# Attention on one core: one pair's bias added by VectorE, norm arguments moved to GpSimd, a set of score products moved ahead of the turned outputs

## The chip, the cores and the metric

The kernel runs on 1 core of one Trainium2 chip. The metric is the device time of one execution in microseconds, as the median of the timed runs. TensorE multiplies matrices into PSUM, VectorE and ScalarE work on PSUM and SBUF, GpSimd on SBUF; SyncE issues DMAs. Each engine runs its own instructions in order, and they meet at semaphores.

## The reference

The input is 32 sequences of 256 tokens with 128 features. Four blocks follow one another, each with a residual: attention with an MLP, a mixture of 8 experts (2 per token), a gated recurrence, and the experts again. The change is in the first block:

```python
xn = _layernorm(x, ln1_g, ln1_b)                 # of an x that is normed already
q, k, v = split(xn @ in_proj_w.T + in_proj_b)    # 16 heads of 8 features
mask = _causal_mask(s, rel_pos)                  # per head: a bias by distance, -inf above the diagonal
scores = einsum('bhqd,bhkd->bhqk', q, k) / sqrt(8) + mask
o = einsum('bhqk,bhkd->bhqd', softmax(scores), v)
x = x + o @ out_w.T + out_b
xm = _layernorm(x, ln2_g, ln2_b)
return x + relu(xm @ w1.T + b1) @ w2.T + b2
```

## The kernel before

The attention block is a software pipeline over the 32 sequences. Every engine has a `body(b)`, written out by hand, that is called for b from -4 to 39; one call is a pass here. The order of calls in it is the order of the engine's instructions, and nothing else sets it. A pass works on several sequences at once: the scores of sequence b, the maxima of b+1, the projections of b+2 and b+3, the output of b-1, the MLP of b-2 and b-3, and the dispatch to experts behind that.

The 16 heads are taken as 8 pairs, j = 0 to 7. A score tile of a pair is 128x768: for each of two heads the three 128x128 blocks on and under the diagonal. Each pair is computed twice:

- **For the maxima.** `bias_for_max` turns the bias into `max_banks` with six 128x128 matmuls, `for_max` adds the products, ScalarE copies the tile to `copied` (`copy_for_max`), and VectorE folds the copies to one maximum per query and head (`fold_keys`, `fold_half`, `fold_on`, `reduce_max`). The maxima go back into q by a DMA.
- **For the scores.** `for_scores` writes `score_banks`, VectorE adds the mask into `ebuf` (`add_mask`, L1153), ScalarE takes the exponential, and `weigh` multiplies by v.

`fill` (L866 and L853 are its first products) issues one pair of scores and one pair of the next sequence's maxima together. There is one `score_banks` and one `max_banks`, so each set waits for the set before to be taken out of both: `scores_free` is raised by VectorE's mask, `maxed_free` by ScalarE's copy. In `fill(b, 0, .., b+1, 3)` the pair for the maxima is number 3; the next set, `fill(b, 1, .., b+1, 4)`, needs that one copied.

`turn(b-1)` (L918, L923) transposes the weighted outputs that ScalarE's `take_O` has copied to `outT`; VectorE's `normalise` (reciprocal L1162, then two products) reads them. TensorE issues it between the third set (scores 2) and the fourth (scores 3).

Three norms run in a pass. For each, VectorE takes `bn_stats` and `bn_aggr`, then the argument var + eps with a small `tensor_scalar` (L1084 and L1085 for the first, L1195 for the second, L1228 for the rows of the experts), and GpSimd raises it to -1/2 (`roots`, `second_root`, `row_root`) and applies it. GpSimd also issues the indirect DMAs that scatter rows to the experts (L1694).

Of the kernel before, what the change touches and what calls it, by code (L numbers as in the profile page):

```python
# [19 lines left out]
P = 128  # L20
# [295 lines left out]
def attention(nc, ctx, s, ins, xres, ident, identb, w, z, region, share, slots_dram, pads_dram):  # L316
# [35 lines left out]
    neghalf = sb("neghalf", [P, 4])  # L352
# [287 lines left out]
    mv = sb("mv", [P, RING, 2, 2])  # L640
    arg = sb("arg", [P, 2, 2])
    rs = sb("rs", [P, RING, 2, 2])
# [23 lines left out]
    stats3, mv3, arg3, rs3 = sb("stats3", [P, 2, 6]), sb("mv3", [P, 2, 2]), sb("arg3", [P, 2]), sb("rs3", [P, 2])  # L666
# [11 lines left out]
    def bankW(lo=0, hi=512):  # L678
# [5 lines left out]
    spread, max_spread = sem("spread"), sem("max_spread")  # L684
    hi_ready, lo_ready, folded, max_ready = sem("hi_ready"), sem("lo_ready"), sem("folded"), sem("max_ready")
    exped, weighed, O_taken = sem("exp_done"), sem("pv_done"), sem("O_taken")
    arg1_ready, rs1_ready, xn_ready, xlb_ready, xl_ready = (sem("arg1_ready"), sem("rs1_ready"), sem("xn_ready"),
                                                            sem("xlb_ready"), sem("xl_ready"))
    arg2_ready, rs2_ready = sem("arg2_ready"), sem("rs2_ready")
    xm_ready, ysum_ready = sem("xm_ready"), sem("ysum_ready")  # L690
    xm_high, arg3_ready, rs3_ready, d_normed = sem("xm_high"), sem("arg3_ready"), sem("rs3_ready"), sem("d_normed")
# [46 lines left out]

    EARLY = 8 + 3

    def banks_of_max(c, j):

        g = 8 * c + j
        return score_banks if g < EARLY and g % 2 == 1 else max_banks

# [20 lines left out]
    with nc.Block() as block:  # L766

        @block.tensor
        def _(pe):
# [45 lines left out]

            def bias_for_max(c, j):
# [3 lines left out]
                max_banks = banks_of_max(c, j)  # L820
# [3 lines left out]
                for hh in range(2):  # L824
                    h = 2 * j + hh
                    nc.tensor.matmul(max_banks[:, hh, 0:P], biasb[:, h, P:2 * P], identb[:], start=True, stop=False,  # L826
                                     skip_group_check=True)
                    nc.tensor.matmul(max_banks[:, hh, P:2 * P], biasb[:, h, 0:P], identb[:], start=False, stop=False,  # L828
                                     skip_group_check=True)
                    nc.tensor.matmul(max_banks[:, hh, 2 * P:BK], biasb[:, h, 0:P], identb[:], start=False, stop=False,  # L830
                                     skip_group_check=True)
# [217 lines left out]
            for b in BODIES:  # L1049
                body(b)  # L1050
# [6 lines left out]
        def _(dve):  # L1057
# [3 lines left out]
            def norm_stats(c):  # L1061
# [6 lines left out]
                if 2 * c in X_PARTS:  # L1068
                    dve.wait_ge(x_in[X_PARTS.index(2 * c)], 16)
# [1425 lines left out]
```

## Time and profile before

| | |
|---|---|
| time, median of 3 runs | 1423.78 us (1423.7 to 1432.5) |
| span of the profiled execution | 1524.2 us |
| granted clock, mean over the span | 0.890 |
| busy, share of the span: TensorE, VectorE, ScalarE, GpSimd | 80%, 75%, 63%, 65% |
| attention loop, first and last reciprocal L1162 | 86.0 and 677.9 us |

The profiled execution has its own time: of it the page gives the span, from the first to the last instruction, and that is longer than the timed runs. The attention loop fills about the first 45% of it; the experts, the recurrence and the experts again follow. An operation's duration in the trace includes its start and its drain, so two neighbours on one engine overlap by some 0.08 us.

### The profile page before, as it was taken

To read this page: it belongs to the slowest core of one execution; us is meant where nothing else is said; L and a number is where in the kernel's file an instruction comes from. 1 tells how busy PE (TensorE), PEld (TensorE's weight loads), DVE (VectorE), ACT (ScalarE), POOL (GpSimd) and SP (SyncE) were. 2 spreads that over 40 slices of the span, in tenths; PEclk is the share of its full clock that TensorE was granted. 3 is DMA by queue.
4 is the path that set the end of the run, shared out by engine and by line. 5 is a ranking of instruction groups with operands and counts; after the bars stand their busy time and mean duration, and the time that the engine had idled before them with its cause. 6 is when DMAs were issued, how large, how long until landed. Compare 5 with 4: busy or idle time off the path is not lost. (4 is left out here: it accounts for less than half of the span.)

```text
span 1524.2 us, 38116 instructions
## 1 busy us (share of the span) xinstructions
PE 1216.6 (80%) x11689; PEld 1017.3 (67%) x11689; DVE 1144.1 (75%) x3833; ACT 967.7 (63%) x2078; POOL 991.9 (65%) x1131
## 2 busy tenths in 40 slices
PE   5889999999999999973788888577787449888850
PEld 3667777777777777753788888455566348788850
DVE  5489999999999999965566665488888546666638
ACT  3588888888888888851555544277777435455420
POOL 4346688888888888777355665237777835666530
PEclk9699999999999999995799997588878669999955
DMA  7211111111111111123222222112222122222228
GB/s 199 86 46 46 48 60 60 60 60 60 59 60 60 60 60 60 39 93 83 73 86 86 81 85 68 49 49 83 73 83 69 45 68 84 86 84 84 77 83 277
DMA packets 99443, 117.19 MB, mean 77 GB/s; under 512 B 17784, under 2 KB 79792, under 8 KB 99248
## 3 DMA queue, kind: packets, MB, share of 16 engines
q1 hardware_dynamic: 70560, 73.57, 16.3%
q0 software_dynamic: 16896, 35.16, 6.8%
q10 hardware_dynamic: 11792, 6.05, 1.4%
q8 instruction: 98, 1.61, 0.5%
q14 instruction: 97, 0.79, 0.2%
HBM read 47.56 MB, written 41.51 MB: 58 GB/s over the span
## 5 line engine op out<-in xcount | busy, mean ns | idle before, releaser
L1153 DVE TENSOR_TENSOR ebuf<-score_banks,region 128x768 f32<-128x768 f32 x256 | 243.6, 951 | 18.8 <-PE score_banks L862 13.1
L1402 ACT ACTIVATE region<-ebuf 128x768 f32<-128x768 f32 x256 | 215.9, 860 | 23.0 <-DVE ebuf L1153 23.0
L1380 ACT CAST copied<-max_banks 128x768 bf16<-128x768 f32 x251 | 201.9, 804 | 15.1 <-PE max_banks L850 12.5
L1842 POOL DMA_INDIRECT choice_rows<-second_yo,second_xg x136 | 133.1, 979 | 112.7 <-PE second_by L1880 69.3
L1842 POOL DMA_INDIRECT choice_rows<-first_yo,first_xg x136 | 130.7, 961 | 114.0 <-PE first_by L1880 65.9
L1694 POOL DMA_INDIRECT expert_rows<-d_rows,a_d_index x112 | 129.4, 1155 | 27.9 <-issue 17.2
L1918 ACT ACTIVATE second_silu<-second_bgu,second_biases 128x256 f32<-128x256 f32 (+1 forms) x144 | 61.0, 466 | 114.3 <-PE second_bgu L1871 66.7
L1918 ACT ACTIVATE first_silu<-first_bgu,first_biases 128x256 f32<-128x256 f32 (+1 forms) x144 | 61.9, 462 | 111.8 <-issue 83.6
L1954 DVE SCALAR_TENSOR_TENSOR second_hT<-second_bgu,second_biases,second_silu 128x256 f32<-128x256 f32 (+1 forms) x144 | 62.1, 464 | 70.3 <-ACT second_silu L1918 37.6
L905 PE MATMUL bankO<-region,vaug 128*32 128x256 f32 (+1 forms) x2048 | 111.1, 334 | 1.9 <-ACT region L1402 1.9
L853 PE MATMUL max_banks<-region_r 32*128 32x256 f32 x502 | 98.3, 388 | 11.9 <-DVE ebuf L1153 7.4
L826 PE MATMUL max_banks<-identb,region 128*128 128x128 bf16 x502 | 100.4, 225 | 4.8 <-ACT copied L1380 4.7
L1954 DVE SCALAR_TENSOR_TENSOR first_hT<-first_bgu,first_biases,first_silu 128x256 f32<-128x256 f32 (+1 forms) x144 | 62.9, 465 | 54.9 <-ACT first_silu L1918 36.1
L866 PE MATMUL score_banks<-region_r 32*128 32x256 f32 x512 | 99.1, 384 | 3.0 <-DVE ebuf L1153 2.9
L1880 PE MATMUL second_by<-region,second_hT 128*128 x544 | 79.3, 289 | 27.4 <-DVE second_hT L1954 23.5
L828 PE MATMUL max_banks<-identb,region 128*128 128x128 bf16 x502 | 99.5, 223 | 0.0
L830 PE MATMUL max_banks<-identb,region 128*128 128x128 bf16 x502 | 99.4, 223 | 0.0
L1880 PE MATMUL first_by<-region,first_hT 128*128 x544 | 82.6, 298 | 17.5 <-DVE first_hT L1954 15.0
L1869 PE MATMUL first_bgu<-first_xhi,first_whi 128*128 128x256 f32 (+1 forms) x288 | 93.5, 325 | 0.6 <-issue 0.6
L1583 POOL TENSOR_TENSOR rs<-arg,neghalf 128x4 f32<-128x4 f32 x32 | 37.1, 1160 | 86.0 <-DVE arg L1085 86.0
L1880 PEld LDWEIGHTS second_by<-region,second_hT 128*128 128x128 f32 x544 | 69.7, 199 | 34.3 <-issue 34.2
L1869 PE MATMUL second_bgu<-second_xhi,second_whi 128*128 128x256 f32 (+1 forms) x288 | 90.5, 314 | 0.4 <-DVE second_xlo L1945 0.2
(369 smaller groups left out, 4531.6 us busy)
## 6 DMA issues: line engine op xcount, KB each, us to landing
region_r<-region_r SPq DMA_DIRECT2D x192, 128.0 KB
first_xg<-expert_rows SPq DMA_DIRECT2D x64, 132.0 KB
second_xg<-expert_rows SPq DMA_DIRECT2D x64, 132.0 KB
z_rows<-choice_rows SPq DMA_DIRECT2D x32, 256.0 KB
c_rows<-choice_rows SPq DMA_DIRECT2D x16, 512.0 KB
out<-xres ACTq DMA_DIRECT2D x16, 256.0 KB
choice_rows<-first_yo,first_xg POOLq DMA_INDIRECT x136
choice_rows<-second_yo,second_xg POOLq DMA_INDIRECT x136
```

Of the source, the lines that this page charges most:

```text
L826: nc.tensor.matmul(max_banks[:, hh, 0:P], biasb[:, h, P:2 * P], identb[:], start=True, stop=False, skip_group_check=True)
L828: nc.tensor.matmul(max_banks[:, hh, P:2 * P], biasb[:, h, 0:P], identb[:], start=False, stop=False, skip_group_check=True)
L905: last = nc.tensor.matmul(bankO[VW * i:VW * (i + 1), g // 2, out:lo + 2 * P], vaug[:, n, kt, h, :], p32[:, (h // 2) % 4, h % 2, cols], sta ...
L1153: nc.vector.tensor_tensor(ebuf[:, half_of_ebuf(c, j), :, :], score_banks[:, :, 0:BK], bias32[:, plain(j), :], ALU.add).then_inc(scores_fre ...
L1380: nc.scalar.copy(copied[:, 2 * j:2 * j + 2, :], banks_of_max(c, j)[:, :, 0:BK]).then_inc(maxed_free, 1)
L1402: nc.scalar.activation(p32[:, j % 4, :, :], ebuf[:, half_of_ebuf(c, j), :, :], ACT.Exp).then_inc(exped, 1)
L1694: pool.indirect_dma_start(slots_dram, bass.IndirectOffsetOnAxis(ap=d.index[:, m % 2, k, t:t + 1], axis=0), d.rows[:, (2 * m + t // 2) % DE ...
L1842: pool.indirect_dma_start(choice_dram, bass.IndirectOffsetOnAxis(ap=xg[:, i % G, t, E:E + 1].bitcast(I32), axis=0), yo[:, i % 4, t, :], No ...
L1869: nc.tensor.matmul(dst, wh[:, at], xhi[:, i % 2, 0:n], start=True, stop=False)
L1880: last = nc.tensor.matmul(by[i % 2][:, t * E:(t + 1) * E], hT[:, i % 4, f, t * P:(t + 1) * P], w["down"][:, bass.ds(e, 1), f, :].rearrange ...
L1918: nc.scalar.activation(act_[:, f, 0:T(i) * P], bgu[i % 2 * NF + f][:, 0:T(i) * P], ACT.Silu, bias=biases[:, i % 4, f:f + 1]).then_inc(silu ...
L1954: nc.vector.scalar_tensor_tensor(hT[:, i % 4, f, 0:T(i) * P], bgu[i % 2 * NF + f][:, 2 * P:(2 + T(i)) * P], biases[:, i % 4, NF + f:NF + f ...
```

## The change

It has three parts. Pair 3 gets its bias for the maxima from VectorE: a table `bias_rows` is made once, TensorE issues no bias matmuls for that pair, ScalarE doesn't copy it, and VectorE's `add_for_max` writes `copied` from the bank and the table. The arguments of the norms move to GpSimd, where `roots` also takes the place of `row_root`. And `fill(b, 3, ..)` is issued ahead of `turn(b-1)`.

```diff
--- before.py
+++ after.py
@@ -349,7 +349,9 @@
-    neghalf = sb("neghalf", [P, 4])
+    MAX_ON_DVE = (3,)
+    bias_rows = sb("bias_by_queries", [P, 2 * len(MAX_ON_DVE), BK], BF16)
+    neghalf = sb("neghalf", [P, 6])
...
@@ -813,22 +823,26 @@
+            def turn_bias(banks, j):
+                for hh in range(2):
+                    h = 2 * j + hh
...
             def bias_for_max(c, j):
 
                 if not exists(c):
                     return
-                max_banks = banks_of_max(c, j)
                 copied = 8 * c + j - 1 if 8 * c + j < EARLY else 8 * c + j
                 if some(copied):
                     pe.wait_ge(maxed_free, copied)
-                for hh in range(2):
...
+                if j not in MAX_ON_DVE:
+                    turn_bias(banks_of_max(c, j), j)
...
@@ -1025,8 +1039,8 @@
                 project_kv(b + 2)
                 mlp_T(b - 2)
                 fill(b, b % RING, 2, b + 1, (b + 1) % RING, 5)
+                fill(b, b % RING, 3, b + 1, (b + 1) % RING, 6)
                 turn(b - 1)
-                fill(b, b % RING, 3, b + 1, (b + 1) % RING, 6)
                 weigh(b, b % RING, 0)
...
@@ -1046,7 +1060,13 @@
+            for q, j in enumerate(MAX_ON_DVE):
+                if q:
+                    pe.wait_ge(rows_taken, q)
+                turn_bias(bankO, j).then_inc(rows_full, 1)
             for b in BODIES:
+                if b == 0:
+                    pe.wait_ge(rows_taken, len(MAX_ON_DVE))
                 body(b)
...
@@ -1076,13 +1098,7 @@
-                    last = ch.mark(nc.vector.bn_aggr(mv[:, n, t, :], stats[:, t, :]))
-                ch.wait(last)
-
-                if some(c):
-                    dve.wait_ge(rs1_ready, c)
-                nc.vector.tensor_scalar(arg[:, 0, :], mv[:, n, :, 1], 1.0, EPS, ALU.mult, ALU.add)
-                nc.vector.tensor_scalar(arg[:, 1, :], mv[:, n, :, 1], 1.0 + EPS, EPS * EPS, ALU.mult, ALU.add).then_inc(arg1_ready, 1)
+                    nc.vector.bn_aggr(mv[:, n, t, :], stats[:, t, :]).then_inc(mv_ready, 1)
...
@@ -1140,6 +1156,19 @@
+            def add_for_max(c, j):
+
+                if not exists(c):
+                    return
+                dve.wait_ge(maxed_full, 8 * c + j + 1)
+                if some(8 * c + j):
+                    dve.wait_ge(maxed_free, 8 * c + j)
+                if some(c):
+                    dve.wait_ge(folded, len(FOLDS) * (c - 1) + fold_of(j) + 1)
+                at = slice(2 * MAX_ON_DVE.index(j), 2 * MAX_ON_DVE.index(j) + 2)
+                nc.vector.tensor_tensor(copied[:, 2 * j:2 * j + 2, :], banks_of_max(c, j)[:, :, 0:BK], bias_rows[:, at, :],
+                                        ALU.add).then_inc(maxed_free, 1)
...
@@ -1301,6 +1327,7 @@
                 fold_half(b + 1, 0)
                 add_mask(b, 0)
                 finish(b - 3)
+                add_for_max(b + 1, 3)
                 members(b - 5)
                 row_stats(b - 3)
                 add_mask(b, 1)
...
@@ -1374,8 +1405,10 @@
                 act.wait_ge(maxed_full, 8 * c + j + 1)
-                g = sum(j >= past for first, past in FOLDS)
-                if some(c) and j == FOLDS[g][0]:
+                if j - 1 in MAX_ON_DVE:
+                    act.wait_ge(maxed_free, 8 * c + j)
...
@@ -1468,7 +1501,6 @@
                 exponentials(b - 1, 7)
-                copy_for_max(b + 1, 3)
                 exponentials(b, 0)
                 copy_for_max(b + 1, 4)
...
@@ -1572,26 +1604,35 @@
+            def roots(c, r):
+
+                n, lo, hi = c % RING, 0 if exists(c) else 2, 4 if exists(r) else 2
+                if exists(c):
+                    pool.wait_ge(mv_ready, 2 * c + 2)
...
+                    ch.mark(nc.gpsimd.tensor_scalar(arg[:, 4:6], mv[:, n, 0:2, 1], 1.0 + EPS, EPS * EPS, ALU.mult, ALU.add))
+                if exists(r):
+                    pool.wait_ge(mv3_ready, 2 * r + 2)
...
+                ch.step(nc.gpsimd.tensor_scalar(arg[:, lo:hi], mv[:, n, lo:hi, 1], 1.0, EPS, ALU.mult, ALU.add))
...
+                nc.gpsimd.tensor_tensor(rs[:, n, lo:hi], arg[:, lo:hi], neghalf[:, lo:hi], ALU.pow).then_inc(rs_ready, 1)
...
@@ -1617,7 +1658,8 @@
-                pool.wait_ge(arg2_ready, c + 1)
+                pool.wait_ge(mv2_ready, 2 * c + 2)
+                ch.step(nc.gpsimd.tensor_scalar(arg2[:], mv2[:, :, 1], 1.0, EPS, ALU.mult, ALU.add))
                 nc.gpsimd.tensor_tensor(rs2[:], arg2[:], neghalf[:, 0:2], ALU.pow).then_inc(rs2_ready, 1)
...
@@ -1726,9 +1761,9 @@
                 biased_input(b - 1)
-                row_root(b - 3)
                 norm_apply(b + 3, (b + 3) % RING)
-                roots(b + 4, (b + 4) % RING)
+                if exists(b + 4) or exists(b - 3):
+                    roots(b + 4, b - 3)
```

TensorE at the start of a pass, from the first set to the bias of the second; before:

```order
L826 MATMUL max_banks<-identb,region 128x128 [waits maxed_free]
L828 MATMUL max_banks<-identb,region 128x128
L830 MATMUL max_banks<-identb,region 128x128
L826 MATMUL max_banks<-identb,region 128x128
L828 MATMUL max_banks<-identb,region 128x128
L830 MATMUL max_banks<-identb,region 128x128
L853 MATMUL max_banks<-region_r 128x256 [waits scores_free,max_spread]
L853 MATMUL max_banks<-region_r 128x256
```

and now, from the same set to the second set's bias:

```order
L867 MATMUL max_banks<-region_r 128x256 [waits scores_free,max_spread,maxed_free]
L867 MATMUL max_banks<-region_r 128x256
L880 MATMUL score_banks<-region_r 128x256 x2
L864 MATMUL max_banks<-region_r 128x128 x2
L876 MATMUL score_banks<-region_r 128x128 x2
L1002 MATMUL bankTW<-w,hT 128x128 x4
L919 MATMUL bankO<-region,vaug 32x256 [waits exp_done]
L919 MATMUL bankO<-region,vaug 32x256 x3
L919 MATMUL bankO<-region,vaug 32x128 x4
L829 MATMUL max_banks<-identb,region 128x128 [waits maxed_free]
```

The first set has lost its six bias matmuls and carries their wait; the bias of the next set still waits for `maxed_free`.

TensorE around the turned outputs (`outT`), before:

```order
L853 MATMUL max_banks<-region_r 128x256 x2
L866 MATMUL score_banks<-region_r 128x256 x2
L850 MATMUL max_banks<-region_r 128x128 x2
L862 MATMUL score_banks<-region_r 128x128 x2
L918 MATMUL bankTW<-ident,outT 128x128 x4
L923 MATMUL bankTW<-ident,outT 128x128 x4
L826 MATMUL max_banks<-identb,region 128x128
L828 MATMUL max_banks<-identb,region 128x128
L830 MATMUL max_banks<-identb,region 128x128
```

and now:

```order
L829 MATMUL max_banks<-identb,region 128x128
L831 MATMUL max_banks<-identb,region 128x128
L833 MATMUL max_banks<-identb,region 128x128
L867 MATMUL max_banks<-region_r 128x256 x2
L880 MATMUL score_banks<-region_r 128x256 x2
L864 MATMUL max_banks<-region_r 128x128 x2
L876 MATMUL score_banks<-region_r 128x128 x2
L932 MATMUL bankTW<-ident,outT 128x128 x4
L937 MATMUL bankTW<-ident,outT 128x128 x4
```

The bias and products of the fourth set stand ahead of the turned outputs.

VectorE from the mask of set 0 to the low part of xm, before:

```order
L1153 TENSOR_TENSOR ebuf<-score_banks,region 128x768
L1202 TENSOR_TENSOR xres<-bankTW,ysum 128x256
L1219 BN_STATS stats<-xres 128x6 x2
L1153 TENSOR_TENSOR ebuf<-score_banks,region 128x768
L1226 BN_AGGR mv<-stats 128x2 x2
L1228 TENSOR_SCALAR arg<-mv 128x2
L1209 TENSOR_TENSOR xmlo<-bankTW,xmhi 128x256
```

and now:

```order
L1182 TENSOR_TENSOR ebuf<-score_banks,region 128x768
L1229 TENSOR_TENSOR xres<-bankTW,ysum 128x256
L1169 TENSOR_TENSOR copied<-max_banks,bias_by_queries 128x768
L1247 BN_STATS stats<-xres 128x6 x2
L1182 TENSOR_TENSOR ebuf<-score_banks,region 128x768
L1254 BN_AGGR mv<-stats 128x2 x2
L1236 TENSOR_TENSOR xmlo<-bankTW,xmhi 128x256
```

The add into `copied` stands behind the finished rows (`xres`) and ahead of the statistics; the argument of the rows is gone.

## Rows read from the trace of the kernel before

**Rows 1.** Stretch table: us; busy of TensorE, its weight loads, VectorE, ScalarE, GpSimd; clock; DMA.

```profile
418.00:456.00 38.00, 35.70 (x474) 28.24 (x473) 35.88 (x100) 33.13 (x62) 33.14 (x41) 1.00 0.18 60
```

**Rows 2.** Waits, 200 to 560 us: who waited for whom, total, times, longest.

```profile
POOL rs L1583 <- DVE arg L1085: 19.1, 19, 1.7
...
PE bankTW L918 <- ACT outT L1411: 11.8, 18, 0.7
```

**Rows 3.** Timeline of VectorE: start, us, line, operation, tiles, [idle before <-releaser].

```profile
426.43 0.48 DVE L1092 SCALAR_TENSOR_TENSOR region_r<-bankTW,bqk,region_r 128x256 fp32r<-128x256 f32 x1 [0.43 <-ACT region_r L1356]
...
428.17 0.41 DVE L1202 TENSOR_TENSOR xres<-bankTW,ysum 128x256 f32<-128x256 f32 x1
...
429.31 0.96 DVE L1153 TENSOR_TENSOR ebuf<-score_banks,region 128x768 f32<-128x768 f32 x1 [0.21 <-PE score_banks L862]
...
430.46 0.47 DVE L1228 TENSOR_SCALAR arg<-mv 128x2 f32<-128x2 f32 x1
431.03 0.42 DVE L1209 TENSOR_TENSOR xmlo<-bankTW,xmhi 128x256 fp32r<-128x256 f32 x1
...
433.10 0.36 DVE L1162 RECIPROCAL rden<-bankTW 128x32 f32<-128x32 f32 x1
...
435.50 0.17 DVE L1084 TENSOR_SCALAR arg<-mv 128x2 f32<-128x2 f32 x1
...
435.65 0.55 DVE L1119 TENSOR_TENSOR fold<-copied 128x768 bf16<-128x768 bf16 x1
...
439.01 0.96 DVE L1153 TENSOR_TENSOR ebuf<-score_banks,region 128x768 f32<-128x768 f32 x1
...
445.64 0.48 DVE L1092 SCALAR_TENSOR_TENSOR region_r<-bankTW,bqk,region_r 128x256 fp32r<-128x256 f32 x1 [0.24 <-ACT region_r L1356]
```

**Rows 4.** Timeline of TensorE, the same pass, same columns.

```profile
428.35 0.23 PE L826 MATMUL max_banks<-identb,region 128*128 128x128 bf16 x1
...
428.79 0.38 PE L853 MATMUL max_banks<-region_r 32*128 32x256 f32 x2
...
431.90 0.66 PE L918 MATMUL bankTW<-ident,outT 128*128 128x128 f32 x4 [0.65 <-ACT outT L1411]
432.39 0.60 PE L923 MATMUL bankTW<-ident,outT 128*128 128x128 f32 x4
...
433.26 0.38 PE L853 MATMUL max_banks<-region_r 32*128 32x256 f32 x2
...
433.63 0.86 PE L905 MATMUL bankO<-region,vaug 128*32 128x256 f32 x16
...
440.52 0.38 PE L853 MATMUL max_banks<-region_r 32*128 32x256 f32 x2
```

**Rows 5.** Timeline of ScalarE, the same pass.

```profile
430.62 0.38 ACT L1421 CAST xmhi<-bankTW 128x256 fp32r<-128x256 f32 x1
...
431.71 0.83 ACT L1380 CAST copied<-max_banks 128x768 bf16<-128x768 f32 x1
```

**Rows 6.** Groups of instructions, VectorE and ScalarE, 200 to 560 us: count, busy, mean.

```profile
L1153 DVE TENSOR_TENSOR ebuf<-score_banks,region 128x768 f32<-128x768 f32 x149 | 141.7, 951 | 6.8 <-PE score_banks L862 3.7 <-ACT region L1402 2.0 <-issue 0.5
...
L1228 DVE TENSOR_SCALAR arg<-mv 128x2 f32<-128x2 f32 x18 | 8.8, 490 | 0.6
...
L1195 DVE TENSOR_SCALAR arg<-mv 128x2 f32<-128x2 f32 x18 | 3.0, 169 | 0.6
...
L1380 ACT CAST copied<-max_banks 128x768 bf16<-128x768 f32 x148 | 119.2, 805 | 1.6
```

**Rows 7.** Timeline of GpSimd, the same pass.

```profile
429.82 1.09 POOL L1694 DMA_INDIRECT expert_rows<-d_rows,a_d_index  x1 [0.18 <-issue]
```

**Rows 8.** Table of stretches, the first passes (clock behind the busy times).

```profile
88.00:92.00 4.00, 2.95 (x44) 1.78 (x41) 3.90 (x11) 2.94 (x4) 2.49 (x3) 0.86 0.02 4
92.00:96.00 4.00, 4.00 (x51) 2.93 (x44) 3.29 (x7) 3.14 (x8) 0.26 (x1) 0.71 0.00 0
```

More of the change, by code:

```diff
@@ L744, in banks_of_max, with fold_of @@
         return score_banks if g < EARLY and g % 2 == 1 else max_banks
+    def fold_of(j):
+        return sum(j >= past for first, past in FOLDS)
     def group(c):
@@ L845, in for_max @@
             def for_max(c, n, j, second):
-                max_banks = banks_of_max(c, j)
+                max_banks, alone = banks_of_max(c, j), j in MAX_ON_DVE
                 for hh in range(2):
@@ L1182, in second_norm @@
                 dve.wait_ge(W_free, useW("att", c) + 1)
+                if some(c):
+                    dve.wait_ge(mv2_ready, 2 * c)
                 for t in range(2):
@@ L1190, in second_moments @@
                 for t in range(2):
-                    last = ch.mark(nc.vector.bn_aggr(mv2[:, t, :], stats2[:, t, :]))
-                ch.wait(last)
-                if some(c):
-                    dve.wait_ge(rs2_ready, c)
-                nc.vector.tensor_scalar(arg2[:], mv2[:, :, 1], 1.0, EPS, ALU.mult, ALU.add).then_inc(arg2_ready, 1)
+                    nc.vector.bn_aggr(mv2[:, t, :], stats2[:, t, :]).then_inc(mv2_ready, 1)
             def finish(c):
@@ L1225, in row_moments @@
                 for t in range(2):
-                    last = ch.mark(nc.vector.bn_aggr(mv3[:, t, :], stats3[:, t, :]))
-                ch.wait(last)
-                nc.vector.tensor_scalar(arg3[:], mv3[:, :, 1], 1.0, EPS, ALU.mult, ALU.add).then_inc(arg3_ready, 1)
+                    nc.vector.bn_aggr(mv[:, row_slot(c), 2 + t, :], stats3[:, t, :]).then_inc(mv3_ready, 1)
             def sort(c):
@@ L1321, in body @@
                 add_mask(b, 4)
+            for q in range(len(MAX_ON_DVE)):
+                dve.wait_ge(rows_full, q + 1)
+                nc.vector.tensor_copy(bias_rows[:, 2 * q:2 * q + 2, :], bankO[:, :, 0:BK]).then_inc(rows_taken, 1)
+            dve.wait_ge(rows_taken, len(MAX_ON_DVE))
             for b in BODIES:
@@ L1376, in copy_for_max @@
                 act.wait_ge(maxed_full, 8 * c + j + 1)
-                g = sum(j >= past for first, past in FOLDS)
-                if some(c) and j == FOLDS[g][0]:
+                if j - 1 in MAX_ON_DVE:
+                    act.wait_ge(maxed_free, 8 * c + j)
+                g = fold_of(j)
+                if some(c) and j == min(i for i in range(*FOLDS[g]) if i not in MAX_ON_DVE):
                     act.wait_ge(folded, len(FOLDS) * (c - 1) + g + 1)
@@ L1652, in residuals @@
                                         xb2[:].rearrange("p t e -> p (t e)"), ALU.add).then_inc(ysum_ready, 1)
-            def row_root(c):
-                if not exists(c):
-                    return
-                pool.wait_ge(arg3_ready, c + 1)
-                if some(c):
-                    pool.wait_ge(d_normed, c)
-                nc.gpsimd.tensor_tensor(rs3[:], arg3[:], neghalf[:, 0:2], ALU.pow).then_inc(rs3_ready, 1)
             def row_apply(c):
```

69 lines of the change are left out of this document (38 added, 31 removed).

## The prediction, made before the changed kernel had run

> **What bounds the kernel now.** I read the table of stretches first, then the waits, then the timelines of the engines over one pass of the attention loop. In the steady stretch no engine stands out: in 38 us TensorE is busy 35.70 us and VectorE 35.88, at a granted clock of 1.00, the 2.4 GHz level [rows 1]. Shares don't say what a microsecond on either is worth, so I looked for the chain that closes from one pass to the next. TensorE waits once a pass for outT, ahead of the turned outputs (18 waits, 11.8 us) [rows 2]; VectorE waits for ScalarE's upper q (0.43 at 426.43) and for the products of set 1 (0.21 at 429.31) [rows 3]. The two hand the chain to each other.
>
> One pass of VectorE [rows 3] and TensorE [rows 4] gives it. Call F the moment at which TensorE starts the products of the pass's second set (L853 at 428.79). Ahead of F, VectorE takes q at 426.43, then come a fold and the mask of set 0, and the finished rows at 428.17. TensorE doesn't wait there: its bias matmuls start at 428.35. Behind F, VectorE adds the mask of set 1 at 429.31 (F+0.52), takes the reciprocal for the turned outputs at 433.10 (F+4.31) and adds the mask of set 5 at 439.01. That ends at 439.97 and releases TensorE's seventh set, from which project_q and the next q follow. The pass takes 19.21 us from q to q (426.43 to 445.64). So what is put into this chain lengthens the pass; time taken off an engine beside it gives nothing.
>
> **The change, part by part.**
>
> *The add on VectorE.* Once a pass ScalarE loses a 128x768 copy (mean 805 ns) and VectorE gains an add of the same shape out of PSUM; the mask add, also out of PSUM, has a mean of 951 ns [rows 6]. Bounds: 0.80 us as the copy, 0.95 as the mask add; I take 0.95, the same engine and operation with one narrower operand and a narrower result. TensorE loses six bias matmuls, 0.44 us from the first to the products (428.35 to 428.79) [rows 4].
>
> What decides is who waits for the add. The bias of the next maxima needs max_banks empty, and it stands ahead of the second set's products in TensorE's queue; queued behind it are k, v, the turned xm and, through these, all that ScalarE does next. The add stands behind the finished rows: it can't start before 428.17 + 0.41 = 428.58, nor end before 429.53. With a hand-over of 0.03 (as from xmhi's end at 431.00 to xmlo at 431.03 [rows 3, 5]) the bias starts at 429.56 instead of 428.35, and F moves to 430.0: **+1.2 us a pass**. With 0.80 us it would be 1.05; nothing or a gain is excluded, since the bias can't start before the bank is read. TensorE's saved 0.44 lies in front of this wait and is worth nothing. VectorE has only row_stats to do meanwhile, then it waits for set 1 too.
>
> *The turned outputs behind the fourth set.* The fourth set's bias needs ScalarE's copy of the maxima of pair 5, which started at 431.71 and took 0.83, so it ended at F+3.75 [rows 5]. ScalarE stands in one row from the values to that copy, all of it behind F, so this moment goes with F. The fourth set can start at F+3.8, its products 0.44 later at F+4.2, and the turn 0.37 after those (433.26 to 433.63, where the next matmuls follow now), at F+4.6. The turn takes 432.39 + 0.60 - 431.90 = 1.09 us [rows 4], to F+5.7, and the reciprocal comes then instead of at F+4.31: **+1.4 us a pass**. Bounds: 0 (if VectorE comes to the reciprocal that late for another reason) and 1.5. VectorE can't do the mask of set 3 first: it stands behind the reciprocal and the outputs. The fourth set itself gains 0.25 us (F+4.47 to F+4.2), and nobody is waiting for that.
>
> *The roots' arguments.* VectorE loses four small operations a pass. The two for the first norm, from 435.50 with the wait ahead of them to the fold at 435.65 [rows 3], lie on the chain: **-0.25** with that wait, 0.15 without. The second norm's lies ahead of the wait for q, which swallows its 0.17. The row argument (L1228) averages 490 ns against 169 for the second norm's of the same shape (L1195) [rows 6]; here it ran from 430.46 to 430.93, and GpSimd's indirect DMA instruction, from 429.82, ended at 430.91 [rows 7]. But what follows it is xmlo at 431.03, and that needs xmhi, which ends at 431.00 [rows 5]. So by the rows it is worth nothing.
>
> The Trainium skill (SBUF — State Buffer, the section on the engine side) says that VectorE and GpSimd share a pair of SBUF ports as an exclusive lock, held for the whole instruction. By that rule the 0.3 us between the two means would be given back, some 10 us in all, and the sum would be about 1478; the rows agree that VectorE was held, but not that anyone waited for it.
>
> GpSimd gains three small operations and loses one pow a pass; it waited 19.1 us for the argument in 19 passes [rows 2], 1.0 a pass, which covers up to 0.3 each. If that cover were gone, the next to be late would be xm, needed behind F, which itself comes later. Cost 0. The one-time bias table is six matmuls and a copy, 0.44 + 0.95 and hand-overs: 0 to 2 us, I take 1. SyncE's queue is untouched.
>
> *Slack.* The mask of set 5 ended at 439.97 and the seventh set's products started at 440.52 [rows 3, 4], so up to 0.5 us of delay is swallowed if TensorE has that reserve in every pass, and 0 if it has none; I take **-0.25**.
>
> *Sum.* 1.2 + 1.4 - 0.25 - 0.25 = 2.1 us a pass. Thirty passes (1 to 30 of 32) have both the add and the turn: 63 us. Four at the ends have only one of them: 2 us. With the table 66 us, so the profiled execution would go from 1524.2 to 1590 us. The median of the timed runs, 1423.78, lies 100 us (7%) under this span. If the loop was as long there, I add 66; if it was shorter in proportion, 62. I take the middle: **1488 us**.
>
> **Rivals.**
>
> *Only the add counts.* If VectorE comes to the reciprocal no earlier than F+5.7, the moved turn costs nothing, and 1.2 is left less the arguments and the slack: 0.7 to 0.95 a pass, 1450 us. Against it: the 3.8 us from the mask of set 1 to the reciprocal are bound to F by TensorE and ScalarE. For it: TensorE's 11.8 us of waits for outT end. Chance 0.14.
>
> *The clock falls.* The new waits (1.6 us at the bias, 1.5 ahead of the fourth set) are longer than the 0.65 of now [rows 4]. In 88 to 92, with TensorE busy 2.95 of 4 us, the clock averaged 0.86, and 0.71 in the next 4 us, so the 1.2 GHz level came in; in 418 to 456 it was 1.00 [rows 1, 8]. The new load would be 35.70/38 of 19.2, so 18.0, less 0.4, in 21.3 us: 83%, between the two. A drop such as that one loses (0.14 + 0.29) x 4 = 1.7 us. If one came every pass and 1 us of it fell on the chain: +30, 1518 us; with all of it 1539. Chance 0.10. The Trainium skill (TensorE: Matmul & The Clock Gate, the section on a second failure mode) describes a loop whose small idles between groups of matmuls let the clock fall and rise again; by it this rival would be the case.
>
> *Not slower: VectorE's own work sets the pace.* This holds if VectorE comes to the add while TensorE is still busy ahead of the second set's bias. Then operations count alone: +0.95 for the add, -0.25, -0.17 and -0.47 for the arguments, about zero: 1424 us; with TensorE's 0.44 a pass gained as well, 1410. The point from which it decides: the add must end before 428.35 - 0.44 = 427.9, while q is taken only at 426.43, two operations of 1.74 us together follow, and then 0.41 and 0.95. So 1.6 us are missing. Chance 0.10. A mixture of these that is neither: 0.04.
>
> **The numbers.** The forecast as worked out has 0.62, and I allow it 1472 to 1504. Reaching down to the first rival and up into the second gives 1446 to 1512, with some 0.2 left outside. A measurement of this kernel tells about 1% from no change (1409.5 and 1438). Faster than that: 0.05; within: 0.08; slower: 0.87.
>
> **What would show it.** In the changed profile: the pass from q to q at 21 to 22 us; TensorE's wait ahead of the bias of the second set, released by VectorE's add, near 1.6 us; its wait ahead of the fourth set's bias, released by ScalarE's copy; VectorE idle ahead of the reciprocal, released by the turn, over 1 us; no wait of VectorE for GpSimd; the clock at 1.00 through the loop. I am wrong if the reciprocal starts straight behind norm_stats, if the add ends before TensorE reaches the bias, or if the clock drops in the loop.

## The result: 1503.5 us, and the profile after

The changed kernel takes 1503.48 us (median of 4 runs, 1502.7 to 1504.37), the kernel before 1424.1 beside it (4 runs, 1423.7 to 1432.5): a ratio of 1.0538, 95% interval 1.0502 to 1.0573. The forecast was 1488, and the range 1446 to 1512 holds the time.

The profiled execution of the changed kernel has a span of 1502.6 us, that of the kernel before 1524.2. That doesn't contradict the times. From the last reciprocal of the attention loop to the end it is 744.8 us now (757.8 to 1502.6), and 846.3 in that one execution before (677.9 to 1524.2). The stretch behind the loop is the same work; 677.9 + 744.8 = 1422.7 is about the median of before. So the loops can be compared directly.

One pass on VectorE, as [rows 3] show it of before (columns: start, duration of one, engine, line, operation, output<-input, how many; in brackets the idle time before it and what ended it):

```profile
475.03 0.48 DVE L1108 SCALAR_TENSOR_TENSOR region_r<-bankTW,bqk,region_r 128x256 fp32r<-128x256 f32 x1 [0.58 <-ACT region_r L1387]
...
477.09 0.95 DVE L1169 TENSOR_TENSOR copied<-max_banks,bias_by_queries 128x768 bf16<-128x768 f32 x1
...
479.07 0.96 DVE L1182 TENSOR_TENSOR ebuf<-score_banks,region 128x768 f32<-128x768 f32 x1 [0.63 <-PE score_banks L876]
...
480.78 0.42 DVE L1236 TENSOR_TENSOR xmlo<-bankTW,xmhi 128x256 fp32r<-128x256 f32 x1 [0.60 <-ACT xmhi L1454]
...
484.37 0.36 DVE L1191 RECIPROCAL rden<-bankTW 128x32 f32<-128x32 f32 x1 [1.48 <-PE bankTW L937]
...
496.34 0.48 DVE L1108 SCALAR_TENSOR_TENSOR region_r<-bankTW,bqk,region_r 128x256 fp32r<-128x256 f32 x1 [0.45 <-ACT region_r L1387]
```

And on TensorE, as [rows 4] of before:

```profile
478.10 0.23 PE L829 MATMUL max_banks<-identb,region 128*128 128x128 bf16 x1 [1.42 <-DVE copied L1169]
...
478.54 0.38 PE L867 MATMUL max_banks<-region_r 32*128 32x256 f32 x2
...
482.35 0.23 PE L829 MATMUL max_banks<-identb,region 128*128 128x128 bf16 x1 [1.35 <-ACT copied L1413]
...
482.79 0.38 PE L867 MATMUL max_banks<-region_r 32*128 32x256 f32 x2
...
483.18 0.66 PE L932 MATMUL bankTW<-ident,outT 128*128 128x128 f32 x4
...
484.20 0.86 PE L919 MATMUL bankO<-region,vaug 128*32 128x256 f32 x16
```

Call F the start of the second set's products again (478.54). From q to F it takes 3.51 us, before 2.36; from F to the reciprocal 5.83, before 4.31. VectorE's add (477.09 to 478.04) ends, and 0.06 us later TensorE starts the bias that waited 1.42 us for it. The fourth set waits 1.35 us for ScalarE's copy of pair 5, the turn follows at F+4.64, and VectorE has stood 1.48 us when its reciprocal starts. At full clock a pass takes 21.31 or 21.72 us in turn, 21.51 in the mean, against 19.18 and 19.58 before: **+2.13 us**.

The waits that stand in [rows 2] of before, in the same stretch of 200 to 620 us (columns: who waited for whom; us in total, times, longest):

```profile
PE max_banks L829 <- ACT copied L1413: 27.1, 20, 1.4
PE max_banks L829 <- DVE copied L1169: 27.0, 19, 1.4
...
DVE rden L1191 <- PE bankTW L937: 31.4, 20, 2.2
...
POOL arg L1615 <- DVE mv L1101: 74.3, 20, 6.4
```

There are 19 to 20 passes in it. TensorE's wait for outT ahead of the turn is gone. In its place are two of 1.4 us a pass, and the reciprocal's wait. GpSimd waits more than before, 3.7 us a pass for VectorE's moments, so it has room for the operations it got.

The whole pass can be read in one row for each kernel. The stretches below reach from one reciprocal to another, over 18 passes of the kernel before and 16 of the changed one (columns: the stretch, its length, then busy time and instructions of PE, PEld, DVE, ACT, POOL, the granted clock, the DMA share, GB/s). Before:

```profile
239.17:588.22 349.05, 328.36 (x4333) 260.26 (x4330) 329.24 (x920) 304.32 (x559) 304.76 (x370) 1.00 0.18 59
```

After:

```profile
223.67:570.41 346.74, 293.44 (x3756) 226.74 (x3752) 288.96 (x769) 258.26 (x481) 265.32 (x360) 0.99 0.16 53
```

TensorE's busy time a pass is 328.36/18 = 18.24 us before and 293.44/16 = 18.34 after. The pass has grown by TensorE's idle time, from 1.15 to 3.33 us. VectorE's busy time hardly changed either (329.24/18 = 18.29 and 288.96/16 = 18.06), so these two rows alone don't say which of the two engines sets the pass; the experiments below do. The clock was 0.99 after, not 1.00 as forecast, and that is the second thing to read. The page has its row of clocks in 40 slices of the span (9 is 90% or more):

```profile
PEclk8679999999999999999986999968999975999985
```

The first three slices, to 113 us, are 8, 6 and 7, and then the loop shows only nines, but a slice of 37.6 us hides a short drop. In the stretch of 86 to 130 us, the mean granted clock is 0.77 now:

```profile
86.00:130.00 44.00, 37.25 (x403) 26.87 (x401) 31.05 (x65) 29.50 (x50) 18.74 (x30) 0.77 0.11 36
```

Before it was 0.96 there:

```profile
86.00:130.00 44.00, 40.03 (x531) 29.58 (x528) 39.87 (x93) 37.84 (x66) 23.90 (x32) 0.96 0.14 46
```

And in the steady loop some passes take 22.8 us from q to q (q at 475.03 came 22.79 after the one before). In these the turn and the weighing behind the bias that waited 1.36 us run at the lower level (1.2 GHz), as here, where the weighing takes 1.51 us and not the 0.86 of 484.20:

```profile
459.56 0.23 PE L829 MATMUL max_banks<-identb,region 128*128 128x128 bf16 x1 [1.36 <-ACT copied L1413]
...
460.87 0.94 PE L937 MATMUL bankTW<-ident,outT 128*128 128x128 f32 x4
461.75 1.51 PE L919 MATMUL bankO<-region,vaug 128*32 128x256 f32 x16
```

### The profile page after: what moved, and what is told of

It is laid out like the page before. It is cut to its first block and busy times, and to the rows that moved or that the text cites. A ratio compares the mean times of both kernels' runs of the same rounds, so it can differ in the third digit from the quotient of the medians.

```text
span 1502.6 us, 37706 instructions
## 1 busy us (share of the span) xinstructions
PE 1166.8 (78%) x11503; PEld 973.0 (65%) x11503; DVE 1141.6 (76%) x3738; ACT 956.2 (64%) x2046; POOL 997.4 (66%) x1216
## 5 line engine op out<-in xcount | busy, mean ns | idle before, releaser
L1413 ACT CAST copied<-max_banks 128x768 bf16<-128x768 f32 x220 | 177.8, 808 | 55.4 <-PE max_banks L864 53.2
L829 PE MATMUL max_banks<-identb,region 128*128 128x128 bf16 x440 | 89.9, 228 | 86.1 <-DVE copied L1169 43.7
L1729 POOL DMA_INDIRECT expert_rows<-d_rows,a_d_index x112 | 122.1, 1090 | 32.0 <-issue 17.1
L919 PE MATMUL bankO<-region,vaug 128*32 128x256 f32 (+1 forms) x2048 | 116.5, 347 | 1.9 <-ACT region L1435 1.9
L1615 POOL TENSOR_SCALAR arg<-mv 128x2 f32<-128x2 f32 x32 | 9.9, 311 | 160.8 <-DVE mv L1101 160.7
L829 PEld LDWEIGHTS max_banks<-identb,region 128*128 128x128 bf16 x440 | 43.9, 100 | 108.5 <-ACT copied L1413 53.8
L1953 ACT ACTIVATE second_silu<-second_bgu,second_biases 128x256 f32<-128x256 f32 (+1 forms) x144 | 66.5, 462 | 53.0 <-issue 28.4
L1989 DVE SCALAR_TENSOR_TENSOR second_hT<-second_bgu,second_biases,second_silu 128x256 f32<-128x256 f32 (+1 forms) x144 | 67.2, 468 | 28.6 <-ACT second_silu L1953 23.1
L831 PE MATMUL max_banks<-identb,region 128*128 128x128 bf16 x440 | 88.8, 226 | 0.0
L833 PE MATMUL max_banks<-identb,region 128*128 128x128 bf16 x440 | 88.7, 225 | 0.0
L919 PEld LDWEIGHTS bankO<-region,vaug 128*32 128x32 f32 x2048 | 57.9, 113 | 42.1 <-issue 12.1
L1906 PE MATMUL first_bgu<-first_xlo,first_whi 128*128 128x256 f32 (+1 forms) x288 | 83.0, 288 | 0.0
```

The source lines that it names most:

```text
L829: nc.tensor.matmul(banks[:, hh, 0:P], biasb[:, h, P:2 * P], identb[:], start=True, stop=False, skip_group_check=True)
L919: last = nc.tensor.matmul(bankO[VW * i:VW * (i + 1), g // 2, out:lo + 2 * P], vaug[:, n, kt, h, :], p32[:, (h // 2) % 4, h % 2, cols], sta ...
L1413: nc.scalar.copy(copied[:, 2 * j:2 * j + 2, :], banks_of_max(c, j)[:, :, 0:BK]).then_inc(maxed_free, 1)
L1729: pool.indirect_dma_start(slots_dram, bass.IndirectOffsetOnAxis(ap=d.index[:, m % 2, k, t:t + 1], axis=0), d.rows[:, (2 * m + t // 2) % DE ...
L1953: nc.scalar.activation(act_[:, f, 0:T(i) * P], bgu[i % 2 * NF + f][:, 0:T(i) * P], ACT.Silu, bias=biases[:, i % 4, f:f + 1]).then_inc(silu ...
L1989: nc.vector.scalar_tensor_tensor(hT[:, i % 4, f, 0:T(i) * P], bgu[i % 2 * NF + f][:, 2 * P:(2 + T(i)) * P], biases[:, i % 4, NF + f:NF + f ...
```

## The experiments

All times are medians, each ratio is to the kernel before on the same chip with its 95% interval. "Pass" is the mean from reciprocal to reciprocal in the steady loop, "work" and "idle" TensorE's busy and idle time in it, from the same kind of row as above. Where the clock in that row is below 1.00 (the change and add_back 0.99, mask_first 0.98, copy5_first 0.93), the work contains slower matmuls.

| kernel | us | ratio | pass | work | idle |
|---|---|---|---|---|---|
| before | 1424.1 | 1 | 19.39 | 18.24 | 1.15 |
| the change | 1503.48 | 1.0538 (1.0502 to 1.0573) | 21.67 | 18.34 | 3.33 |
| turn_back | 1458.5 | 1.0186 (1.0132 to 1.024) | 20.45 | 18.02 | 2.42 |
| add_back | 1463.94 | 1.0255 (1.0212 to 1.0298) | 20.74 | 18.70 | 2.04 |
| args_only | 1423.24 | 0.9963 (0.993 to 0.9996) | 19.29 | 18.30 | 0.99 |
| add_early | 1422.25 | 0.9954 (0.9934 to 0.9973) | 19.27 | 18.14 | 1.12 |
| busy_waits | 1492.42 | 1.047 (1.0446 to 1.0494) | 21.51 | 20.15 | 1.35 |
| mask_first | 1503.69 | 1.054 (1.0514 to 1.0567) | 21.94 | 18.63 | 3.31 |
| both_mended | 1455.94 | 1.0212 (1.0182 to 1.0243) | 20.35 | 18.36 | 1.99 |
| all_mended | 1447.0 | 1.0145 (1.0118 to 1.0173) | 20.08 | 18.32 | 1.76 |
| copy5_first | 1547.15 | 1.0853 (1.0819 to 1.0886) | 22.97 | 19.64 | 3.33 |
| out_early | 1414.69 | 0.9935 (0.9912 to 0.9957) | 18.98 | 18.13 | 0.85 |
| old_out_early | 1419.94 | 0.9946 (0.9924 to 0.9969) | 19.26 | 18.40 | 0.86 |
| out_early_2 | 1414.93 | 0.9927 (0.99 to 0.9953) | 18.98 | 18.13 | 0.85 |

### One part taken back at a time

**turn_back**: the change without its third part.

```diff
+                turn(b - 1)
                 fill(b, b % RING, 3, b + 1, (b + 1) % RING, 6)
-                turn(b - 1)
```

> The change with the turned outputs back ahead of the fourth set; the add on VectorE and the moved arguments stay. Theory (two new waits in one chain): the reciprocal comes 1.4 us earlier again, the pass falls from 21.5 to about 20.1 us, the wait ahead of the second set's bias stays at 1.4 us; with the clock's falls gone as well, 1445 to 1458 us. Rival (only the add counts, the moved turn is free): 1495 us or more, VectorE's idle time ahead of the reciprocal turning up elsewhere.

**add_back**: the change without its first part; ScalarE copies pair 3 again.

```diff
-    MAX_ON_DVE = (3,)
+    MAX_ON_DVE = ()
...
-                add_for_max(b + 1, 3)
...
+                copy_for_max(b + 1, 3)
                 exponentials(b, 0)
```

> The change with pair 3 back on TensorE and ScalarE (bias matmuls and copy as before); the moved turn and the moved arguments stay. Theory: the wait ahead of the second set's bias goes, 1.2 us a pass with it; 1.4 of the turn less 0.25 for the arguments and 0.25 of slack stay: a pass of 20.3 us, 1450 to 1458 us. Rival (only the add counts): 1415 to 1424 us.

**args_only**: both taken back, so that only the roots' arguments are moved.

> Only the roots' arguments moved to GpSimd; the bias and the order of TensorE's sets as before the change. Theory: the first norm's two arguments lie on the chain, the other two are covered: 0 to 0.25 us a pass, 1416 to 1424 us. Rival (VectorE is the bound and the held argument counts): 1.0 us a pass, about 1392 us. Rival (GpSimd becomes late): over 1430 us.

In turn_back TensorE's waits show the add alone:

```profile
PE max_banks L829 <- DVE copied L1169: 29.8, 21, 1.4
...
PE bankTW L932 <- ACT outT L1444: 13.8, 21, 0.7
```

That is 1.42 us ahead of the second set in each of 21 passes, and the old wait for outT of 0.66. The pass is 20.45, where about 20.1 was expected, so the add with the arguments costs 1.06 us, and the moved turn on top of it another 1.06 (21.51 - 20.45). The time lies 0.5 us above the upper end of what was expected. From the reciprocal to the next q it takes 12.56 and 12.68 us in turn (436.02 to 448.70 in the pass that was read), 12.7 in the mean before. In args_only, which has neither the add nor the moved turn, it is 12.6 as well. So the 0.1 us goes with the arguments, and the reserve of 0.25 us that the prediction subtracted isn't there.

In add_back the undisturbed pass is 20.56 to 20.63, some at up to 22.0 with the clock down; it is 0.3 us above what was expected, and the time 6 us: the turn alone, less the arguments, costs 1.2 us. TensorE waits 1.33 us for the copy of pair 5, VectorE 1.57 for the turn. Taken singly, the parts cost 1.06 and 1.2 us, each less 0.1 for the arguments, which makes about 2.5 without them; together they cost 2.13 + 0.1. So they overlap by some 0.2 us.

args_only gives 0.10 us a pass, not 0.25. The row of its loop (18 passes) has VectorE busy for 311.23/18 = 17.29 us a pass, a whole 1.00 us less than before:

```profile
233.53:580.68 347.15, 329.36 (x4333) 261.56 (x4330) 311.23 (x847) 302.98 (x559) 301.06 (x406) 1.00 0.18 60
```

What VectorE saves ends in its waits:

```profile
DVE xmlo L1228 <- ACT xmhi L1441: 13.2, 22, 0.6
DVE ebuf L1174 <- PE score_banks L874: 12.1, 42, 0.4
```

VectorE now stands 0.6 us a pass ahead of xmlo until xmhi is there, where the profile of before lists no wait, and some 0.55 us for TensorE's scores, where it was 0.2 (4.3 us in 20 waits). So an engine that is 94% busy (329.24 of 349.05) gave up 1.00 us of work a pass, and the pass became 0.10 us shorter: these operations don't set it. The Trainium skill (SBUF — State Buffer, the section on the engine side) has VectorE and GpSimd share a pair of ports as an exclusive lock, and by that rule the prediction had 0.3 us of the row argument's time come back. That operation is off VectorE here, with the other three, and the pass is 0.1 us shorter in all, so at most that much can be its share.

### The place of the add

**add_early**: the add directly behind the lower q, the finished rows and the fold behind the add, the turn in its old place.

```diff
                 take_q(b + 2)
-                fold_half(b + 1, 0)
+                add_for_max(b + 1, 3)
                 add_mask(b, 0)
                 finish(b - 3)
-                add_for_max(b + 1, 3)
+                fold_half(b + 1, 0)
```

> The change with the turn back ahead of the fourth set and the add moved forward on VectorE: straight behind the taking of q, ahead of the mask of set 0, with the fold behind the finished rows. Theory (not the add's 0.95 us but its place costs): it ends at 427.8 on the old scale, before TensorE reaches the second set's bias; the mask of set 0 then ends at 428.65 and F stays at 428.8; VectorE is late by 0.7 us at set 1 and level again at xmlo; pass 19.1 to 19.4 us, 1412 to 1426 us. Rival (VectorE is full and the add's length counts wherever it stands): a pass of 20.0 us or more, 1443 us and up.

All of the 1.06 us is gone: pass 19.27, and TensorE issues the second set's bias (443.96, with no idle time ahead of it) behind an add that starts 0.40 us behind q (442.77), where it was 2.06 in the changed kernel.

```profile
442.37 0.48 DVE L1108 SCALAR_TENSOR_TENSOR region_r<-bankTW,bqk,region_r 128x256 fp32r<-128x256 f32 x1 [0.21 <-ACT region_r L1387]
442.77 0.95 DVE L1169 TENSOR_TENSOR copied<-max_banks,bias_by_queries 128x768 bf16<-128x768 f32 x1
```

```profile
443.96 0.23 PE L829 MATMUL max_banks<-identb,region 128*128 128x128 bf16 x1
```

So the add's 0.95 us on VectorE cost nothing where they fit. Its place in VectorE's queue did.

### The clock

**busy_waits**: the changed kernel with sixteen extra matmuls of the identity ahead of the two new waits, into a bank that has been emptied; no result of the kernel uses them.

```diff
             def bias_for_max(c, j):
...
+                if c >= 2 and j in (4, 6):
+                    pe.wait_ge(O_taken, 2 * c - 3)
+                    for k in range(16):
+                        nc.tensor.matmul(bankO[:, 0, 0:P], identb[:], identb[:], start=True, stop=True)
```

> The changed kernel with sixteen 128x128 products of the identity put on TensorE ahead of the bias of pairs 4 and 6, that is into its two waits of 1.42 and 1.35 us (sixteen products of the weighing take 0.86 us in its trace). They go into a bank that has been emptied, and no other result changes. Theory (the clock pays for the new waits): the passes of 22.8 us among those of 21.3 and 21.7 go, with them the early stretch at a lower clock, and the time falls by 8 to 16 us to 1487 to 1496. Rival (the long passes have another cause): they stay, 1500 to 1508. If the added products end later than the waits, every pass grows: over 1510.

The first theory holds: 1492.42. All steady passes are 21.31 or 21.71, and in the early stretch the clock is 1.00 where the changed kernel had 0.77:

```profile
86.00:130.00 44.00, 38.99 (x539) 29.54 (x538) 35.12 (x76) 33.40 (x59) 21.75 (x34) 1.00 0.14 46
```

The extra matmuls take 1.07 us and leave 0.42 and 0.36 us of the waits:

```profile
444.86 1.07 PE L845 MATMUL bankO<-identb 128*128 128x128 bf16 x16
446.34 0.23 PE L829 MATMUL max_banks<-identb,region 128*128 128x128 bf16 x1 [0.42 <-DVE copied L1173]
...
449.17 1.07 PE L845 MATMUL bankO<-identb 128*128 128x128 bf16 x16
450.59 0.23 PE L829 MATMUL max_banks<-identb,region 128*128 128x128 bf16 x1 [0.36 <-ACT copied L1417]
```

The passes at full clock are as long as in the changed kernel, so about 11 us of the change's 79 are the clock (1503.48 - 1492.42). By the Trainium skill (TensorE: Matmul & The Clock Gate, the section on a second failure mode) small idles between groups of matmuls make the clock fall and rise again; the runs agree, with 0.77 against 1.00 in one stretch. Why it is only some of the steady passes that lose it, no run here shows.

### What the moved turn costs

The prediction put the turn's price on VectorE: it comes to the reciprocal late. **mask_first** is the changed kernel with the mask of set 3 ahead of the reciprocal.

```diff
-                normalise(b - 1)
                 add_mask(b, 3)
+                normalise(b - 1)
```

> The changed kernel with VectorE's mask of set 3 ahead of its reciprocal instead of behind it, so that VectorE does 0.95 us of work while it waits 1.48 us for the turned outputs. Theory (the move of the turn costs because VectorE takes its queue in order and stands): the pass falls from 21.5 to 20.6 to 20.9 us, 1473 to 1485. Rival (what is late is TensorE's own chain through the copy of pair 5, and VectorE's wait is only its shadow): the pass stays at 21.4 to 21.6, 1496 to 1508.

The rival holds. At full clock a pass of this kernel on VectorE reads:

```profile
276.30 0.48 DVE L1108 SCALAR_TENSOR_TENSOR region_r<-bankTW,bqk,region_r 128x256 fp32r<-128x256 f32 x1 [0.44 <-ACT region_r L1387]
...
284.59 0.96 DVE L1182 TENSOR_TENSOR ebuf<-score_banks,region 128x768 f32<-128x768 f32 x1 [0.42 <-PE score_banks L876]
285.65 0.36 DVE L1191 RECIPROCAL rden<-bankTW 128x32 f32<-128x32 f32 x1
...
298.01 0.48 DVE L1108 SCALAR_TENSOR_TENSOR region_r<-bankTW,bqk,region_r 128x256 fp32r<-128x256 f32 x1 [0.58 <-ACT region_r L1387]
```

VectorE fills its wait with a mask (284.59) and goes on to the reciprocal without idle time, 9.35 us behind q. In the changed kernel it is 9.34 (475.03 to 484.37), and q to q is 21.71 here. The wait of 1.48 us was a shadow. What counts is on TensorE: behind the turn everything in its queue is later, the weighing at F+5.66 (484.20) where it was at F+4.84 before (433.63 to 428.79 in [rows 4]). As the rows read, the turn and the wait of 0.65 for outT filled the time until the copy of pair 5 was done; now TensorE stands idle for it and does the turn afterwards. (The mean of 21.94 and the time come from more passes at the lower clock, 0.95 in 480 to 620 us; why this kernel has more of them is open.)

**both_mended**: the whole change, with the add of add_early and the mask of mask_first.

> The whole change, with VectorE's order fitted to it: the added bias right behind the lower query instead of behind the mask of set 0, and the mask of set 3 ahead of the reciprocal. Theory (places on VectorE cost what the change cost, not its operations): pass 19.1 to 19.6, 1415 to 1430, as the kernel before or a little under. Rival (set 3's bias still waits for ScalarE's copy of pair 5, and the turn behind it): pass 19.9 to 20.4, 1440 to 1458.

Again the rival, 1455.94: with both places on VectorE mended, the turn in its new place still costs some 34 us (1455.94 against 1422.25 in add_early), and TensorE still waits for the copy of pair 5, 1.21 us a pass:

```profile
PE max_banks L829 <- ACT copied L1413: 25.4, 21, 1.3
```

**all_mended**: the same, and ScalarE's copy of the outputs, which stood ahead of the copy of pair 5, moved up to a place where ScalarE is idle.

```diff
+                take_O(b - 1, 1)
                 exponentials(b, 0)
                 copy_for_max(b + 1, 4)
...
-                take_O(b - 1, 1)
                 copy_for_max(b + 1, 5)
```

> The whole change with VectorE's order fitted (the added bias behind the lower query, the mask of set 3 ahead of the reciprocal; 1456, pass 20.27), and ScalarE's copy of the outputs' second half moved up to ahead of the exponential of set 0. That copy takes 0.6 us and stood ahead of the copy of pair 5, for which TensorE waits 1.29 us ahead of set 3. Theory (the moved turn costs because it no longer fills TensorE's wait for the copy of pair 5): that wait falls to about 0.7 and the pass to 19.6 to 19.8, 1434 to 1444. Rival (the turn costs 1.0 us by its place ahead of the weighing, whatever TensorE waits): pass 20.1 to 20.4, 1450 to 1460.

Between the two, 1447.0. Counted from the upper q (L1387), the copy of pair 5 comes 5.32 and 5.50 to 5.58 us later in turn, instead of 5.70; in some passes it now waits 0.2 us for its own input. TensorE's wait for it falls from 1.21 us a pass to 0.89, its idle time by 0.23, and the pass by 0.27. That is no cheaper turn, though: out_early below makes the same move without the moved turn, and its pass falls by 0.29. From there to all_mended, the moved turn and VectorE's order for it cost 20.08 - 18.98 = 1.10 us; from add_early to both_mended it was 20.35 - 19.27 = 1.08, and behind the late add 1.06. Much of that price can be read in TensorE's waits, all in 200 to 620 us. all_mended waits ahead of the fourth set:

```profile
PE max_banks L829 <- ACT copied L1413: 18.7, 21, 0.9
```

out_early waits ahead of the turn:

```profile
PE bankTW L932 <- DVE xmlo L1236: 6.5, 22, 0.3
```

That is 0.89 us a pass in place of 0.30. In the other pair it is 1.21 in both_mended in place of 0.60 in add_early (12.6 us in 21 waits). The wait that the moved turn opens is 0.6 us longer each time than the one that it closes, somewhat more than half of its price; where the rest comes from is not shown.

**copy5_first**: all_mended with the copy of pair 5 directly behind that of pair 4.

```diff
                 copy_for_max(b + 1, 4)
+                copy_for_max(b + 1, 5)
                 take_values(b + 2)
                 take_xmT(b - 2)
                 take_upper_k(b + 2)
-                copy_for_max(b + 1, 5)
```

> The kernel of the run with the early outputs and the fitted order, with the copy of pair 5 moved up as well, to directly behind the copy of pair 4, so that TensorE finds set 3's maxima bank empty. Theory (TensorE's work of 18.2 us a pass and its waits make the pass): the wait of 1.29 us ahead of set 3 is gone, pass 18.8 to 19.2, 1400 to 1418, with the turn in its new place. Rival (values, the high part of xm and the upper keys come 0.8 us later behind that copy, and VectorE and TensorE then wait for those): pass 19.6 to 20.4, 1430 to 1458.

Far off both, 1547.15. The chain of waits can be read. ScalarE comes to the copy before pair 5 is computed and waits itself:

```profile
481.39 0.80 ACT L1413 CAST copied<-max_banks 128x768 bf16<-128x768 f32 x1 [1.10 <-PE max_banks L864]
...
482.35 0.39 ACT L1454 CAST xmhi<-bankTW 128x256 fp32r<-128x256 f32 x1
```

xmhi ends late for that, VectorE stands ahead of xmlo with the mask of set 2 behind it, and TensorE stands for that mask:

```profile
482.77 0.42 DVE L1236 TENSOR_TENSOR xmlo<-bankTW,xmhi 128x256 fp32r<-128x256 f32 x1 [1.80 <-ACT xmhi L1454]
```

```profile
484.55 0.38 PE L867 MATMUL max_banks<-region_r 32*128 32x256 f32 x2 [1.79 <-DVE ebuf L1182]
```

I had counted what the copy releases and what it delays, and not whether its own input was there. The clock is down here too (0.93), so the three times of 1.1 to 1.8 us don't add up to the pass by themselves.

### A version that beats both

**out_early**: add_early (turn in its old place) with the outputs' copy moved up as in all_mended.

> The version with the added bias behind the lower query and the turn in its old place (1422 before), with ScalarE's copy of the outputs' second half moved up from behind the upper keys to ahead of the exponential of set 0, a place where ScalarE waits 1.6 us for VectorE and the copy takes 0.6. Theory (TensorE's wait of 0.60 us ahead of the turn is on the path): the pass falls from 19.27 to 18.7 to 19.0 us, 1400 to 1414. Rival (VectorE's queue, 95% busy, sets the pass by itself): 1417 to 1426.

**old_out_early**: the kernel before with nothing but that move. **out_early_2**: out_early once more, beside it.

> The kernel before with nothing of the change, and only ScalarE's copy of the outputs' second half moved up to ahead of the exponential of set 0. It asks whether the gain of the run with the early outputs needs the change. TensorE works some 18.2 us a pass there and waits 1.1, of that 0.65 for this copy. Theory (TensorE's work and waits make the pass): 18.8 to 19.1 us, 1402 to 1418, as with the add on VectorE. Rival (without the add and the moved arguments VectorE or ScalarE takes TensorE's place as the limit): 19.3 to 19.5, 1420 to 1430.

> The version with the add behind the lower query, the turn in its old place, the moved arguments and the early outputs once more, on the same chip as the kernel before with the early outputs alone. Theory: the two lie within 0.4% of each other, 1405 to 1420, since TensorE's waits are the same. Rival (the change's own operations are worth something once their places fit): this one is lower by 0.5% or more.

out_early is the fastest: 1414.69 and 1414.93, 0.9935 and 0.9927 of the kernel before. The wait ahead of the turn is 0.30 us instead of 0.60, and now it is for VectorE:

```profile
482.99 0.63 PE L932 MATMUL bankTW<-ident,outT 128*128 128x128 f32 x4 [0.30 <-DVE xmlo L1236]
```

So half of the wait was to be had, and the pass fell by 0.29, to 18.98, as expected. The time is 0.7 us above the upper end of what was expected. The old kernel with the same move missed its expectation: its passes alternate between 18.93 and 19.58, 19.26 in the mean, at the same idle time of TensorE (0.86), and it takes 1419.94. In the pass lengths the change's own operations, with their places fitted, are worth 0.28 us, and 0.27 of it is TensorE's work (18.40 against 18.13). The times of the two, from one chip, differ by 5.0 us or 0.35%, which is inside the 0.4% of the theory, and the two intervals overlap (0.99 to 0.9953 and 0.9924 to 0.9969), so the times alone don't settle it.

## Why the prediction was right, point by point

- **Add on VectorE, +1.2 us a pass.** Right: F moved by 1.15, the wait is 1.42 (forecast about 1.6), and the pass of turn_back grew by 1.06 with the arguments in it. That the place decides and not the 0.95 us is shown by add_early.
- **Turn behind the fourth set, +1.4.** The times were right to 0.1 us (copy of pair 5 ready for the set at F+3.81, forecast 3.8; turn at F+4.64, forecast 4.6; reciprocal at F+5.83, forecast 5.7). Its price was 1.06 behind the add, and the step from the late reciprocal to the late pass was wrong: mask_first filled VectorE's wait and gained nothing. The path is TensorE's own queue. The prediction closed its chain over VectorE's mask of set 5 and TensorE's seventh set; the line at 440.52 in [rows 4] carries no idle time, so TensorE came to that set from work of its own.
- **Arguments, -0.25.** Mis-sized: 0.10 (args_only). Other waits of VectorE took up nine tenths of the 1.00 us that it was spared.
- **Slack, -0.25.** Not there with the add alone (12.56 and 12.68 us from reciprocal to q against 12.7, as much as the arguments account for). In the change that stretch is 0.56 us shorter (11.97 and 12.36), but this is the same mistake seen from the other side: the reciprocal came 1.5 us later and TensorE's queue only 0.8 to 1.1, so the distance shrank. So the terms for the arguments and the slack took off 0.15 and 0.25 us too much, and the turn's term had put in 0.34 too much (1.4 against 1.06).
- **Sum, +66.** At full clock it holds: first to last reciprocal takes 651.6 us in busy_waits against 591.9 before, +59.7; the first reciprocal comes 4.4 later (90.4 against 86.0); together 64. That it holds so closely is luck in part: the errors of the three terms just named cancel to 0.06 us a pass.
- **The clock at 1.00 through the loop.** Wrong, and the greater part, 11 us, of the 15 by which the time lies above the forecast. The rival "the clock falls" had the mechanism and took it for every pass or none; it came in the early passes and in 5 of some 25 steady ones, 11 us in all.
- **Not slower, only the add.** Both excluded. TensorE waits 1.42 us for the add, and with the turn taken back the time falls by 45 us (1503.48 to 1458.5). add_early shows what the first of them needed, an add that ends before TensorE reaches the bias. (The 1.74 us that the prediction puts down to two operations behind q run from the start of q to the finished rows and contain q itself; its 1.6 us are right.) **GpSimd at 0, TensorE's saved 0.44 worth nothing.** Right: with its places unmended the change left TensorE idle for 2.2 us more a pass than before, and VectorE never waits for GpSimd for the arguments.

## What to carry to other kernels

Before costing a move, divide the steady loop by passes and read the busy time and the idle time of each engine. Work plus waits makes the pass on every engine, so the sum alone doesn't name the one that counts; taking work off an engine does. Here 1.00 us off VectorE gave 0.10, and filling its wait ahead of the reciprocal gave nothing. out_early, with 0.27 us less of TensorE's work than old_out_early, has a pass shorter by 0.28, though its edit touches VectorE too. TensorE's work of 18.0 to 18.4 us was nearly the same in every kernel at full clock without added matmuls. The changes to the pass were the waits that opened or closed on TensorE. Work that happens to stand in a wait is a filler: before moving it, ask what wait it covers.

## What the runs showed of the hardware

The clock can fall in a loop in which no wait of TensorE that the profile lists is longer than some 1.4 us (200 to 620 us): with 293.44 us busy of 346.74 the mean was 0.99 and single passes lost about 1.1 us. In the early passes (37.25 busy of 44) it was 0.77. With the idle times filled up to 0.42 us (38.99 busy of 44, and 322.46 of 344.13 in the loop) it was 1.00 in both. So useless matmuls in a wait made this kernel 0.7% faster. One such wait need not bring the clock down: turn_back has 1.42 us of it in each pass, and its steady loop ran at 1.00 with no pass above 20.51 us.
